# A chunk pipeline written out by hand: where the next chunk's normalisation, two transposes, a halo copy and a weight split stand among their neighbours

## The reference, cut to what matters

```python
# block 1, on x normalised twice
xk, xv, xr = (xn * m + shift(xn) * (1 - m) for m in (mix_k, mix_v, mix_r))   # shift: the token before
k, v, sr = xk @ Wk.T, xv @ Wv.T, sigmoid(xr @ Wr.T)
x = x + (sr * wkv(time_decay, time_first, k, v)) @ Wo.T     # wkv: a scan over the tokens
xn2 = layer_norm(x)
kf = square(relu(mix(xn2) @ Wk_ffn.T))                      # 256 -> 1024
x = x + sigmoid(mix(xn2) @ Wr_ffn.T) * (kf @ Wv_ffn.T)      # 1024 -> 256
# block 2, on the normalised result of block 1
shared = (gelu(xf @ w1s) * (xf @ w2s)) @ w3s
expert = argmax(xf @ Wg)
out = x1 + layer_norm(shared + (gelu(xf @ W1[e]) * (xf @ W2[e])) @ W3[e])
```

## Time and profile before

| | |
|---|---|
| median of 3 runs | 1054.4 us (1046.81 to 1061.86) |
| the profiled execution, its time on the device | 1044.21 us |
| its span, first to last instruction | 1042.5 us |
| mean granted TensorE clock | 0.97 of full speed |
| busy: PE, PEld, DVE, ACT, POOL | 90%, 80%, 71%, 57%, 56% of the span |

### The profile page before, as it was taken

One profiled execution on the slowest core, in us unless ns is written; L12 is line 12 of the kernel. 1 busy time (PEld: TensorE's weight loads), 2 busy tenths in 40 slices (PEclk: granted clock), 3 DMA queues, 4 the chain that ended last, 5 costly groups with the idle time before them and its releaser, 6 DMA issues.

```text
span 1042.5 us, 28016 instructions
## 1 busy us (share of the span) xinstructions
PE 935.1 (90%) x9734; PEld 838.8 (80%) x9734; DVE 735.0 (71%) x1653; ACT 591.6 (57%) x1014; POOL 589.0 (56%) x800
## 2 busy tenths in 40 slices
PE   2366899999999999999999999869999999999994
PEld 1255788888878878878878887758999999999994
DVE  5887999999988988989889886432444444444442
ACT  5375787787777777776777774423333333333331
POOL 5346468567667667567567542443554554555453
PEclk9688999999999999999999999989999999999998
DMA  6111350351251350340343146566777788485510
GB/s 232 61 52 55 97 198 23 127 203 50 94 204 29 112 199 21 123 182 30 131 161 131 64 171 201 208 229 214 264 225 239 251 268 272 147 281 190 179 58 22
DMA packets 87339, 156.37 MB, mean 150 GB/s; under 512 B 5549, under 2 KB 68142, under 8 KB 82160
## 3 DMA queue, kind: packets, MB, share of 16 engines
q1 hardware_dynamic: 35760, 72.74, 20.3%
q10 hardware_dynamic: 46960, 65.89, 19.5%
q0 software_dynamic: 4560, 16.98, 4.2%
HBM read 178.35 MB, written 50.51 MB: 220 GB/s over the span
## 4 chain that ended last, share of the span: by engine, by line
PE 51%; DVE 16%; POOL 13%; issue 8%; ACT 6%; DMA 2%; ACTq 2%; SPq 1%; POOLq 0%; DVEq 0%
PE up L342 10%; PE up L344 10%; PE up L343 10%; PE yp L549 4%; PE yp L342 4%; PE yp L344 4%; PE yp L343 4%; PE yp L546 4%; POOL inv L1479 3%; DVE mixed L1006 2%; POOL inv L1466 2%; POOL sh_s L1547 2%; DVE stats L987 1%; ACT L769 1%; DVE arena L981 1%
## 5 line engine op out<-in xcount | busy, mean ns | idle before, releaser
L342 PE MATMUL up<-mix_s,arena 128*128 128x128 f16 x1248 | 211.1, 219 | 2.3 <-DMA arena<-w_split 1.8
L344 PE MATMUL up<-mix_s,arena 128*128 128x128 f16 x1248 | 211.1, 219 | 0.0
L343 PE MATMUL up<-mix_s,arena 128*128 128x128 f16 x1248 | 211.1, 219 | 0.0
L342 PE MATMUL up<-xf_s,arena 128*128 128x256 f16 x512 | 140.4, 274 | 5.5 <-issue 4.5
L344 PE MATMUL up<-xf_s,arena 128*128 128x256 f16 x512 | 140.5, 274 | 0.0
L343 PE MATMUL up<-xf_s,arena 128*128 128x256 f16 x512 | 140.4, 274 | 0.0
L1648 POOL TENSOR_TENSOR kf_s<-ex,kf_s 128x512 f16<-128x512 f32 x78 | 90.1, 1156 | 86.4 <-ACT kf_s L940 86.3
L1419 DVE SCALAR_TENSOR_TENSOR ex<-up,ex 128x512 f32<-128x512 f32 x78 | 53.9, 691 | 103.2 <-ACT ex L934 102.9
L342 PEld LDWEIGHTS up<-mix_s,arena 128*128 128x128 f16 x1248 | 122.0, 98 | 2.9 <-DMA arena<-w_split 1.9
L343 PEld LDWEIGHTS up<-mix_s,arena 128*128 128x128 f16 x1248 | 122.0, 98 | 0.4
L344 PEld LDWEIGHTS up<-mix_s,arena 128*128 128x128 f16 x1248 | 122.0, 98 | 0.0
(11 more groups left out here) (228 smaller groups left out, 2904.2 us busy)
## 6 DMA issues: line engine op xcount, KB each, us to landing
arena<-w_split ACTq DMA_DIRECT2D x117, 1024.0 KB
arena<-in_W SPq DMA_DIRECT2D x24, 1024.0 KB, 6.0
w_split<-arena SPq DMA_DIRECT2D x24, 1024.0 KB, 10.2
rows<-routed_rows ACTq DMA_DIRECT2D x39, 261.0 KB, 2.9
routed_rows<-x_in SPq DMA_DIRECT2D x8, 650.0 KB, 6.4
normed<-routed_rows ACTq DMA_DIRECT2D x39, 128.0 KB, 2.5
x_in<-in_x SPq DMA_DIRECT2D x16, 256.0 KB, 2.8
x_res<-in_x SPq DMA_DIRECT2D x16, 256.0 KB, 2.7
```

The lines of the kernel that those rows point to most:

```text
L342: pe.matmul(out, stat(0), mov(0), start=first, stop=False)
L343: pe.matmul(out, stat(0), mov(1), start=False, stop=False)
L344: return pe.matmul(out, stat(1), mov(0), start=False, stop=last)
```

## The change

Six pieces of code move; no instruction is added or taken away.

1. PE: `channel_mix_up(0)` and `(1)` stand before `transpose_next` instead of behind it.
2. ACT: `ln0(i + 1)` stands behind `exps(1)`, `own(1)` and the two Gelus instead of before `exps(1)`.
3. ACT: `xnT_norm` stands behind the second `relu_up` instead of before the first.
4. DVE: the late expert split stands behind `shared(0)` and `shared(1)` instead of before `kept`.
5. DVE: the halo of `xnT` stands behind `num`, just before `divide`, instead of behind `den_now`.
6. DVE: `own(3)` (a split of an own weight, in steps 1 and 2 alone) stands before `placing` and the halo of `xn2T`, and in steps 0 to 2 `distances` stands before both.

```diff
@@ PE
                 shared_up(1)
+                channel_mix_up(0)
+                channel_mix_up(1)
                 transpose_next()
-                for q in range(4):
-                    channel_mix_up(q)
+                channel_mix_up(2)
+                channel_mix_up(3)
@@ ACT
                 receptance()
-                if not at_step(i, -1):
-                    ln0(i + 1, 1 - p)
                 exps(1)
                 own(1)
                 gelu(0)
                 gelu(1)
-                xnT_norm()
+                if not at_step(i, -1):
+                    ln0(i + 1, 1 - p)
                 relu_up(0)
...
                 square(0)
                 relu_up(1)
+                xnT_norm()
                 square(1)
@@ DVE
                     tops(c0)
+                early = isinstance(i, int) and i <= 2
+                if on(c0) and early:
+                    distances(c0)
+                own(3)
...
                     halo(xn2T, c1, 1 - p, "halo2", "xn2T")
-                if on(c0):
+                if on(c0) and not early:
                     distances(c0)
-                own(3)
...
-                late_lo(last_late(i, p, h))
                 if on(c0):
                     kept(c0)
                     scan_b(c0)
                     scan_a(c0)
                 shared(0)
                 shared(1)
+                late_lo(last_late(i, p, h))
...
                 own(0)
-                if on(i + 1):
-                    halo(xnT, i + 1, 1 - p, "halo", "xnT")
...
                     den_r(c0)
                     num(c0)
+                if on(i + 1):
+                    halo(xnT, i + 1, 1 - p, "halo", "xnT")
+                if on(c0):
                     divide(c0)
```

## The result

The changed kernel takes **1025.8 us** (median of 4 runs, 1024.4 to 1027.1), where the kernel before took 1055.5 (1046.8 to 1061.9) on the same chip: a ratio of 0.972, with an interval of 0.965 to 0.980. The forecast was 1032 with a range from 1019 to 1045. The profiled execution after took 1025.36 us, with a span of 1023.5; the one before took 1044.21, with a span of 1042.5. From span to span of the two profiles the gain is 19.0 us (1.8%), and not the 29.7 between the medians; the forecast's sum was 22.1.

A forecast was written before the change was run, and what follows sets the result against it. PE was taken to bound the steady steps, with DVE bounding odd steps after the change. Terms of -8, 0, -12.8 and -1.3 (step 15) sum to -22.1: 1022 us, or 1032 with the 10.2 offset; range 1019 to 1045.

The forecast's parts named there:

- Steps 0 to 2: Beginning of the run: 0.85 from the halo, 3.9 in step 1, 3.4 in step 2, together -8 us (5 to 10).
- Steps 3 to 14: Looped steps: 0 over steps 3 to 6 and -12.8 us over steps 7 to 14.
- the forecast's odd step: Odd looped steps: bound by DVE, 38.8 us long, with a gap of about 2 us before `w_k`.
- the wait for PE at `x3_gate`: DVE in even steps: there at 348.3, before PE's product at 350.0, so it waits; even step 37.1 us.
- The stores: SP issues both stores some 1.9 us later; up to 2 us on ACT, which has 3 to spare: no cost.
- Rival C: PE's clock falls at the new gap before `w_k`; even steps take 38.5 us, total 1041; chance 0.15.
- Rival F: Slower: more POOL operations fall on busy DVE, +2.9 us per odd and +2.4 per even step; total 1069; chance 0.05.
- The offset of 10.2 us: Whole run: the median of the kernel before lay 10.2 us above its profiled execution; the same was added to 1022.

The follow-up runs named there:

- after_again: The changed kernel itself, unaltered, measured again on one chip beside the kernel before and other variants: 1026.9 us, ratio 0.979.
- first_splits_only: The kernel before with only item 6, `distances` ahead of `own(3)` in steps up to 2: 1041.0 us, ratio 0.993.
- ln0_only: The kernel before with only item 2, `ln0` behind the Gelus on ACT: 1029.3 us, ratio 0.984.
- late_split_back: The changed kernel without item 4, the late split back ahead of `kept` and the scans: 1023.8 us, ratio 0.979.
- halo_back: The changed kernel without item 5, the halo of `xnT` back ahead of `gate`, `den_r` and `num`: 1029.8 us, ratio 0.985.
- low_halves_first: The changed kernel with POOL making the first two low halves of `sh` before it issues the scatter: 1026.6 us, ratio 0.979.

## Why the prediction was right, and where it was not

**The end result** lies in the range and is faster by 2.8% (2.0 to 3.5%), which had a chance of 0.48. The 2.8% owe something to luck, since three of the four runs of the kernel before took over 1054 us here, as only 4 of 27 did later: beside after_again it is 2.1% (1.5 to 2.7%), and from profile to profile 1.8%. The main mechanism came as forecast: PE no longer waits for Gelu 0, nor the Gelus for `ln0` and POOL's inverse, and DVE bounds the odd steps. But two errors of opposite sign partly cancelled, and the account of what each part gives was poor.

- **Steps 0 to 2**: -8 forecast, with 5 to 10; -9.85 measured (127.00 to 117.15). first_splits_only shows -9.0 of it by item 6 alone. Steps 0 and 1 gave 5.05 for 4.75; step 2 gave 4.8, where I took 3.4 between 2.0 and 5.3.
- **Steps 3 to 14**: -12.8 forecast, -6.5 measured. The mis-sized term is one: "from `x3_gate` to the next `w_k` it took 6.7". Up to that point the forecast's odd step was exact: DVE at `x3_gate` 32.16 us behind the step's `w_k`, and 379.90 - 347.69 = 32.21 in the profile after. That is partly luck: the first two pairs of `mixed` take 2.14 + 1.77 us, 0.46 more than the 0.78 + 2.67 of step 7, and a CAST of 128x2 values before them takes 0.17 instead of 0.61. From there on it takes 387.22 - 379.90 = 7.3 us, in even steps too. Step 7, from which I had the 6.7, had one POOL operation on its last pair of `mixed` (1.77 us); now there are two in each step (2.67). I carried the collisions of step 7 over although the change moves all that they depend on. An odd step became 39.5 instead of 38.8 (the forecast's own sum gives 38.86), an even one 37.5 instead of 37.1. In even steps the wait for PE at `x3_gate` failed too: DVE was to be there 28.2 us behind the step's start and PE's product at 29.9; it comes at 340.36 - 310.18 = 30.2 and finds the product ready, since the collisions on the first two pairs have used up the wait.
- **Items 1 to 3** are called one edit in the forecast ("go together"). ln0_only shows that item 2 is most of the gain and that items 1 and 3 on top of it cost 5.6 us, item 3 at least in part by the halo's wait for `xnT_norm`, which the forecast left out of the sum. I had computed that `ln0` ends at 296.0 and `shared_up(1)` at 296.1, so the numbers for this were in my own text, and I did not put them side by side.
- **Item 4** was to keep DVE from holding the Gelus' products. late_split_back shows that it costs 0.9 us in each odd step, and gains only in step 15: 617.61 - 578.79 = 38.8 against 40.2 without it and 40.1 before, the 1.3 us forecast.
- **Item 5**: `delta` beside the reciprocal was free, as forecast (3.34 us kept). I left out that POOL's scatter and first low half move back with it, onto `mixed`: 2.14 for 0.78. Without it the kernel is 3 to 4 us slower, but not by the steady steps, where it gives in even steps (the halo's wait of 1.86 us) what it takes in odd ones. The saving forecast for the beginning came: in steps 0 and 1 `num` takes 0.69 us each in the profile after, and 1.53 in halo_back as before.
- **The stores** cost nothing: ACT's split at the end of step 9 starts without a wait.
- **Rival C, the clock**: it stays at 1.00 from 100 to 600 us in spite of gaps of 1.65 us before `w_k` in every second step. What the clock cost before was overestimated, but not in the sum: the forecast put 1.8 us of step 7 on it, and step 13 with the same gap before `w_fk` and no fall took 40.5 us, 0.9 less. **Rival F**'s mechanism (more collisions, since DVE no longer idles) is the one that took the missing 6 us, at a fifth of its price: it had steps 3 to 14 at 31.8 us above the forecast's.
- **Behind step 15** nothing was forecast. Of the 19.0 us between the two spans 1.4 lie there, less than the 2.2 by which the changed kernel's two profiles differ in that stretch.
- **The offset of 10.2 us** between profile and median was the second error. It belonged to the first runs of the kernel before and not to this work: after it is 0.4. Without it the forecast would have been 1022, 4 us too low; with it, it was 6 us too high. Why the runs of the kernel before spread over 20 us and those of the changed one over 4 isn't settled. first_splits_only, which keeps PE's wait for Gelu 0, spreads over 10.7 us in 10 runs, and the kernels without that wait over at most 6.2 in 4 or 5, which speaks for a clock that falls behind that gap more often in some runs than in others. The profiles say that this is too small by itself: in the profile before, the clock falls (to 0.91, 0.95 and 0.93 over 20 us) behind three of the four gaps of 2.29 us in the loop, and these odd steps take 41.2 to 41.4 us; behind the fourth it stays at 1.00, and the step takes 40.5. In first_splits_only it falls behind one of four (41.2 us against 40.4 and 40.5). A fall costs 0.7 to 0.9 us, and four of them under 4.

**How the parts add up.** In medians (us): before 1045.7 on the chips of these kernels; item 2 -16.6; items 1 and 3 +5.6; item 6 -4.5; item 5 -3 to -4; item 4 +2 to +3. That makes 1028 to 1030, and the changed kernel took 1025.8 and 1026.9. In profiled executions: 1044.2 - 10.8 + 2.7 - 6.9 - 4.2 + 1.9 = 1026.9, and the changed kernel's took 1025.4 and 1028.2. Items 2 and 6 alone would by these sums come at 1025 to 1027, as the whole change does, and with a POOL order fitted to them perhaps lower; this wasn't tried.

## What to carry to other kernels

When a wait is taken off one engine, price the next engine with its neighbours as they will stand then: the collisions of two engines are a matter of a microsecond's shift, and a carried-over count is a guess. Of an edit that "goes together" with another, compute both alone; here one of the six pieces gave 16.6 of the some 20 us, and the one that was moved along with it made a new wait. Once two engines contend, look for work of the one that can run beside instructions of the other that don't mind (here the reciprocal), and check that it doesn't hold back a transfer that the next stage waits for. And take a profiled execution's distance to the median as a property of those runs until a second kernel shows it.

## What the runs showed of the hardware

- **A collision of DVE and POOL has no fixed price.** A pair of `mixed` takes 0.78 us alone, 1.77 with one POOL operation on it and 2.67 with two, which is the 0.9 to 1.0 each that I counted on. Where a low half follows right on the end of the scatter, one pair takes 2.14, 1.36 more than alone. And with the end of the scatter's descriptors and two back-to-back `mix_lo` beside them (2.27 us together), a copy of 0.16 us took 2.64 and a product of 0.69 took 3.52. In step 9 each held pair ends 0.28 or 0.29 us behind the POOL operation that held it: 377.68 behind 377.39, 379.98 behind 379.70, 383.89 behind 383.61. The Trainium skill (SBUF — State Buffer, "two separate sides") has whichever of the two starts first hold the shared port pair for the whole instruction, and the other fully blocked, where DVE's instruction has two SBUF inputs and POOL's reads SBUF, or where DVE's is in a two-port mode. These numbers agree that DVE is blocked and not slowed, and go further: the wait lasted through two instructions. It is the same the other way round, where POOL's product of 128x2 values took 5.69 us before beside a DVE that worked without a break, and takes up to 3.5 after. Not every overlap costs: in low_halves_first the pair that starts at 371.59 and two operations of 0.68 and 0.69 us ran beside the scatter's two issues in 0.87, 0.68 and 0.69 us; a pair with nothing beside it takes 0.87 in ln0_only too.
- **The reciprocal is beside it all.** It took 3.34 or 3.35 us in every kernel here, whatever POOL did: `delta`, the scatter's descriptors or two low halves of `sh`. The Trainium skill (SBUF — State Buffer, "Who interferes with whom") says that a DVE instruction with at most one SBUF input, outside its two-port modes, does not contend; the runs agree.
